# Who forms the first trial value of a threshold search, and where ScalarE's small copies stand

## What is computed

```python
def _top_p_attention(X, W1, W2, W3):
    q = X @ W1.T @ W2.T
    k = X @ W3.T
    probs = softmax(q @ k.T, axis=-1)                   # 4096 x 4096
    idx = argsort(-probs); sp = take_along_axis(probs, idx)
    keep_sorted = cumsum(sp) - sp < 0.9                 # the smallest set with 0.9 of the mass
    A = probs * mask                                    # mask: keep_sorted, put back in place
    return A / maximum(A.sum(-1), 1e-12)

R = (S + eye) / (S + eye).sum(-1)                       # S is adj
for n in range(2):
    A = _top_p_attention(Xa, W1, W2, W3)
    Xf = R @ Xf
    Xa = A @ Xa
    Z = Z + Xf @ U1[n].T + Xa @ U2[n].T
out = layernorm(x + layernorm(X + Z) * ln_g + ln_b)
```

## Time and profile before

| | us |
|---|---|
| median of 3 runs (4349.74 to 4353.28) | 4351.58 |
| the profiled execution | 4350.77 |
| its span | 4349.0 |
| busy in the span: TensorE | 3762.5 (87%) |
| VectorE | 3623.6 (83%) |
| ScalarE | 3114.5 (72%) |
| GpSimd | 1017.3 (23%) |

### The profile page before, as it was taken

One profiled execution on the slowest core, in us unless ns is written; L12 is line 12 of the kernel. 1 busy time (PEld: TensorE's weight loads), 2 busy tenths in 40 slices (PEclk: granted clock), 3 DMA queues, 4 the chain that ended last, 5 costly groups with the idle time before them and its releaser, 6 DMA issues.

```text
span 4349.0 us, 66313 instructions
## 1 busy us (share of the span) xinstructions
PE 3762.5 (87%) x25364; PEld 3163.1 (73%) x25364; DVE 3623.6 (83%) x6400; ACT 3114.5 (72%) x3128; POOL 1017.3 (23%) x1412
## 2 busy tenths in 40 slices
PE   8677877777777769999999749999999999999996
PEld 5677777777777747777778547777777777778875
DVE  2899999999999939888888188888888889999995
ACT  3789889898989845555555367777777777777771
POOL 0000000000000000001010224444444445555555
PEclk9899999999999989999999979999999999999998
DMA  3211111111111020000000212222233423333332
GB/s 116 93 45 66 45 55 56 47 64 47 64 47 64 27 78 12 19 16 19 16 17 17 87 35 85 87 83 88 88 93 93 134 90 105 107 107 105 100 104 73
DMA packets 131759, 292.49 MB, mean 67 GB/s; under 512 B 14122, under 2 KB 94186, under 8 KB 127058
## 3 DMA queue, kind: packets, MB, share of 16 engines
q1 hardware_dynamic: 131410, 287.99, 20.6%
HBM read 250.19 MB, written 37.75 MB: 66 GB/s over the span
## 4 chain that ended last, share of the span: by engine, by line
PE 34%; ACT 28%; DVE 14%; issue 14%; POOL 10%; DMA 1%; DVEq 0%; SPq 0%; ACTq 0%; POOLq 0%
PE ps L803 11%; PE ps L642 9%; DVE b L1226 7%; ACT b L871 6%; ACT b L988 5%; ACT b L989 5%; DVE b L1173 3%; ACT b L865 3%; PE ps L792 3%; ACT b L971 3%; PE ps L748 3%; PE ps L623 2%; POOL b L468 2%; ACT b L859 1%; PE ps L780 1%
## 5 line engine op out<-in xcount | busy, mean ns | idle before, releaser
L707 PE MATMUL ps<-b 128*128 128x257 f32 x4096 | 902.1, 379 | 0.0
L803 PE MATMUL ps<-b 128*128 128x257 f32 x4096 | 900.9, 379 | 0.0
L642 PE MATMUL ps<-cb,b 128*128 128x128 f32 x4096 | 606.9, 312 | 321.7 <-ACT b L865 321.7
L707 PEld LDWEIGHTS ps<-b 128*128 128x128 f32 x4096 | 775.6, 189 | 118.3 <-issue 3.8
L803 PEld LDWEIGHTS ps<-b 128*128 128x128 f32 x4096 | 770.2, 189 | 111.7
L642 PEld LDWEIGHTS ps<-cb,b 128*128 128x128 f32 x4096 | 546.1, 163 | 371.1 <-ACT b L865 329.6
L1137 DVE SCALAR_TENSOR_TENSOR b<-b 128x4096 f32<-128x4096 f32 x128 | 566.4, 4425 | 63.1 <-ACT b L859 59.8
L1139 DVE CUSTOM_DVE_ANT_0 b<-b 128x4096 f32<-128x4096 f32 x128 | 566.3, 4425 | 5.5 <-DMA b<-in_adj 1.1
L871 ACT ACTIVATE b<-ps 128x1024 f32<-128x1024 f32 x512 | 499.9, 1023 | 75.6 <-PE ps L642 74.0
L623 PE MATMUL ps<-b 128*64 128x128 f32 x8192 | 504.0, 276 | 0.0
L865 ACT ACTIVATE b<-b 128x4096 f32<-128x4096 f32 x128 | 474.4, 3706 | 8.0 <-DVE b L1141 8.0
(11 more groups left out here) (186 smaller groups left out, 4743.2 us busy)
## 6 DMA issues: line engine op xcount, KB each, us to landing
b<-in_adjTb SPq DMA_DIRECT2D x256, 512.0 KB, 3.8
b<-in_adj SPq DMA_DIRECT2D x32, 2048.0 KB, 8.0
y_d<-b SPq DMA_DIRECT2D x64, 128.0 KB, 1.7
h_d<-b SPq DMA_DIRECT2D x64, 128.0 KB, 1.8
b<-h_d SPq DMA_DIRECT2D x64, 128.0 KB, 2.3
b<-in_xT SPq DMA_DIRECT2D x1, 4096.0 KB, 15.8
b<-in_x SPq DMA_DIRECT2D x32, 128.0 KB, 2.2
b<-y_d SPq DMA_DIRECT2D x32, 128.0 KB, 2.1
```

Of the source, the lines that this page charges most:

```text
L642: last = nc.tensor.transpose(bank(2 * (gq % 3), 2)[:, b * 128:(b + 1) * 128], ub[:, u % UB, j * 128:(j + 1) * 128], ident_s)
L707: last = mm(b[:, 0:XA], aj[:, q % AJR, e, :], xf[:, j, :], start=False, stop=(j == NT - 1))
L803: last = mm(o[:, 0:XA], at[:, q % ATR, b, :], xa[:, j, :], start=(j == 0), stop=(j == NT - 1))
```

## The change

Three things, all in the second step:

- VectorE forms the product of the two bounds (`bracket_head`: three operations on 128x1), after the sixth level of tile `n` and ahead of the final rows' statistics; it waits for `e8` there and signals `bh`. With the `max` in it the choice between the two cases of the bracket is made in two operations.
- GpSimd's `bracket` begins with the root, once `bh` is there. Its own product (L474) goes. The bounds and the factors are computed after the root, as before. VectorE waits for the root (`bt`) ahead of L1232.
- ScalarE starts level 1 right after the exponentials; `av_ev` and `mq_ev` come between level 1 and level 2.

```diff
+LEAST = (1 - TOP_P) / 4096 / 1.0001
...
                 def bracket(t):
                     a = lambda i: ptm[:, i:i + 1]
                     Z = zE[:, t % 2:t % 2 + 1]
-                    po.wait_ge(g["e8"], t + 1)
+                    po.wait_ge(g["bh"], t + 1)
+                    m = tst[:, t % 2:t % 2 + 1]
+                    tt(m, m, ahalf, ALU.pow).then_inc(g["bt"], 1)
                     h7, g7 = e8[:, 7:8], am[:, 8:9]
                     ts(a(0), Z, TOP_P, None, ALU.mult)
...
-                    plink(tt(a(8), a(6), a(4), ALU.mult))
-                    tt(tst[:, t % 2:t % 2 + 1], a(8), ahalf, ALU.pow).then_inc(g["bt"], 1)
                     plink(tt(a(7), a(6), mone, ALU.pow))
...
-                def acts(t, items):
+                def acts(t, items, n):
                     items = list(items)
                     for k in range(1, ACT_LEVELS + 1):
                         if t < NT:
                             level(t, k)
+                        if k == 1:
+                            if 1 <= n <= NT:
+                                av_ev(n - 1)
+                            if n >= 2 or n + 2 < NT:
+                                mq_ev(n - 2 if n >= 2 else None, n + 2 if n + 2 < NT else None)
...
-                    if 1 <= n <= NT:
-                        av_ev(n - 1)
-                    if zm:
-                        mq_ev(tz, tx)
...
+                def bracket_head(t):
+                    Z = zE[:, t % 2:t % 2 + 1]
+                    ve.wait_ge(g["e8"], t + 1)
+                    link(v.scalar_tensor_tensor(out=x_, in0=Z, scalar=TOP_P, in1=am[:, 8:9], op0=ALU.mult,
+                                                op1=ALU.is_le))
+                    link(v.scalar_tensor_tensor(out=x_, in0=Z, scalar=LEAST, in1=x_, op0=ALU.mult, op1=ALU.max))
+                    v.tensor_scalar(tst[:, t % 2:t % 2 + 1], x_, e8[:, 7:8], None, ALU.mult).then_inc(g["bh"], 1)
...
                         if t == 0:
+                            bracket_head(0)
                             ve.wait_ge(g["bf"], 1)
...
+                        if t + 1 < NT:
+                            bracket_head(t + 1)
                         final_stats(t)
+                        if t + 1 < NT:
+                            ve.wait_ge(g["bt"], t + 2)
                         link(v.scalar_tensor_tensor(out=VN, in0=E, scalar=mid, in1=E, op0=ALU.is_le,
                                                     op1=ALU.mult, accum_out=G))
```

More of the change, by code:

```diff
@@ L273, in gat_topp_kernel @@
                       "gd", "po", "rd", "xs", "acc", "nz", "hi", "gi", "yd", "ys", "fi", "fa", "s1", "f1", "s2",
-                      "fo", "fd", "lv", "lr", "lt", "qd", "e8", "bt", "bf", "xc"):
+                      "fo", "fd", "lv", "lr", "lt", "qd", "e8", "bt", "bf", "xc", "bh"):
                 g[n] = sem(f"{n}_{s}")
@@ L468, in bracket @@
                     ts(a(1), h7, -1.0, 1.0, ALU.mult, ALU.add)
-                    plink(ts(a(2), Z, (1 - TOP_P) / 4096 / 1.0001, None, ALU.mult))
+                    plink(ts(a(2), Z, LEAST, None, ALU.mult))
                     ts(a(3), g7, a(0), None, ALU.is_ge)
@@ L1059, in _ @@
                         expo(n + 1)
-                    if 1 <= n <= NT:
-                        av_ev(n - 1)
-                    if zm:
-                        mq_ev(tz, tx)
[L1064 to L1067, removed]
+                    if s == 0:
+                        if 1 <= n <= NT:
+                            av_ev(n - 1)
+                        if zm:
+                            mq_ev(tz, tx)
+                        if tx is not None:
+                            gx_ev(tx)
+                    else:
+                        acts(n + 1, [2 * p + i for p in pairs_in(n) for i in range(2)], n)
                 barrier(ac, kS[s])
```

## The result

| | before | after |
|---|---|---|
| median of 5 runs, us | 4350.14 (4348.73 to 4353.28) | 4376.96 (4374.4 to 4378.75) |
| span of the profiled execution, us | 4349.0 | 4375.2 |
| ratio, 95% interval | | 1.0058 (1.0046 to 1.0070) |

The changed kernel is 0.6% slower. I had forecast 4340 us in a range of 4325 to 4370; the first rival, the lost race, stood at 4370, and the time lies 7 us above both.

The account below looks back on a forecast made before the run. No engine is full, so a loop of waits bounds the kernel (late, GpSimd's arrival at the reduction). Early -34 and late +22 give -12 us: 4339 from the profiled 4350.8, 4340 as median, range 4325 to 4370.

Parts of the forecast that it names:

- the first rival: Late periods: GpSimd's power operation L481 starts behind VectorE's L1232 and takes 6.45 us, not 2.31; +31, 4370 us; chance 0.22.
- the slower rival: Same as the first rival: late, L481 falls behind L1232, 12 periods cost 4.25 us instead of 1.9; 4370 us, chance 0.22.
- the early gain: Early periods: -5.6 + 1.6 + 2.1 = -1.9 us each, over 18 periods -34 us.
- root's path: Early: with VectorE's head and GpSimd's root first, ScalarE's levels start 1.64 us behind the exponentials, not 7.21; -5.6 us.
- copies: Early: ScalarE's three copies, free under the wait for the root, come onto the loop behind level 1; +1.6 us per period.
- ScalarE's stall: Early: ScalarE waits for the factors ahead of L995 because GpSimd is stopped by L1232; +2.1 us per period.
- the earlier trace: Rows of one late period before the change where L481 took 6.45 us; the forecast counted its loss as regained, -2.4 us.
- GpSimd stopped behind the root: Early: GpSimd's second small operation behind the root is held until VectorE's L1232 ends, taking more than 4 us.
- TensorE not the bound: Early: TensorE needs at most 53.3 us per period, less than the new period of 54.7.
- the border period: The period between the early and late regimes, where ScalarE was just last; +0.5 us.
- the late copy behind level 1: Late: the product's copy (L1010) delays GpSimd's L492 from 9.96 to 11.9 us behind the exponentials; +1.9 us, 12 periods, +23.
- The fast rival: Early: GpSimd isn't stopped behind the root, factors come in time; -58 to -72 instead of -34, 4302 to 4316 us; chance 0.1.

Follow-up runs that it names:

- e1: The changed kernel with two small VectorE operations added ahead of L1252 in the late turns; 4342.7 us.
- e7: The changed kernel with one small VectorE operation added ahead of L1252 in the late turns; 4337.8 us.
- e2: The changed kernel with the three ScalarE copies back ahead of level 1, leaving only the new way to the root; 4324.2 us.
- e6: The changed kernel with the three copies back ahead of level 1 and two small VectorE operations ahead of L1252 in the late turns; 4296.8 us.
- run 12: Not a follow-up run: part of the phrase "a race run 12 times", the race of L482 and L1252 in the last 12 periods.
- e3: The kernel before with only the three ScalarE copies moved behind level 1; 4425.9 us.
- e5: The changed kernel with VectorE, in turns before 17, starting L1252 only after GpSimd's signal just ahead of the power operation; 4358.7 us.
- e4: The kernel before with one more small GpSimd operation at the head of the bracket in the late turns; 4372.8 us.
- e8: e6 with GpSimd's search levels (its reduction) moved ahead of its work on the final rows; 4301.5 us.

## Why the prediction was wrong

**The step that failed** is the one in the slower rival, "By my sum L481 starts 4.25 us behind the start of the third head operation, and L1232 4.29", from which I had L481 just ahead. In the rows above it is 4.40 and 4.29 (L1222 3750.94, L482 3755.34, L1252 3755.23). VectorE's side was exact, and the root started at +0.30 as worked out. From the root to the power operation it took 4.10, not 3.95 us, and 0.11 of that lies in one place: the operation behind the root came 0.64 us after its start (3751.24 to 3751.88), where 0.53 stood between L475 and its follower in before. (With 0.53 the spacings of the row in before add up to the 3.95.) A sum of a dozen spacings was asked to decide an order by 0.04 us, and was 0.15 off. A margin that small gives near even odds, not 0.22. My range also ended at the rival's own number, 4370, and left nothing for an error in it. With the race won, by e1 and e7, the kernel takes 4342.7 and 4337.8 us, on both sides of my 4340; against the runs of before beside them that is 7 and 15 us faster, where I had forecast 12.

**The size of the rival.** It was put at 4370 and came out at 4377. The loop started 1.7 us later, where I had 0.6, but only 0.49 of that is the head's; the early gain was 31.1, not 34 (root's path -5.7, copies +1.7, ScalarE's stall +2.4, where I had -5.6, +1.6 and +2.1); and a late period lost 4.6 us instead of 4.25. One reading was off: in the earlier trace rows the factors came 2.2 us later behind the last exponential (by the start of L492, 12.15 against 9.96); 2.4 is their delay behind L1232's own start, which was 0.2 sooner there.

**Right:** the root's path, 0.92 us to the root and 1.50 to the levels (forecast 1.64 for the latter); GpSimd stopped behind the root, 4.53 us, though at its first small operation and not its second; early periods 54.96 us in the mean where I said 54.7; TensorE not the bound; the border period, +0.6 for +0.5; the late copy behind level 1, which e1 shows alone as L493 at 11.96 (forecast 11.9) and +1.8 us a period (forecast 1.9); the loss passing on to the reduction and VectorE's wait. The fast rival fell, since the stop behind the root came in every early period.

**What I didn't see.** First, GpSimd is held until the end of VectorE's operation whether the race is won or lost, so that winning it is worth the 2.3 us of the power operation at most. Second, the copies are better left where they were: I charged them 1.6 us early and took their place for needed; e2 and e6 show that ScalarE has the room, 4296.8 us against e1's 4342.7.

The row for the first, timeline of before, a late period, to be read with the earlier trace rows:

```profile
3771.30 2.19 POOL L482 TENSOR_SCALAR b<-b 128x2 f32<-128x2 f32 x1
```

L482 ends 0.09 us behind the end of L1232.

**Open:** why the operation behind the root comes after 0.64 us and not 0.53. In before the follower was a second power operation (L476), here it is a TENSOR_SCALAR (L470); no run varied it. Also open are the 0.6 us between GpSimd's arrival at the reduction and the answer (e1).

## What to carry to other kernels

Where two engines start long operations within some tenths of a microsecond and one of them can stop the other, treat the order as a term of its own: look for it in all periods of the trace, ask which edits upstream shift either side, and make it safe with an explicit wait or a cheap delay of the side that wins nothing by being early. Before work is moved off a wait that hides it, work out what the wait becomes once the thing waited for is sooner: here ScalarE still had to wait, only further down. Test the parts of a change by themselves: here one part alone gains 26 us, the other costs 46 to 76, and a tenth of a microsecond, in a race run 12 times, another 34.

## What the hardware showed

**A GpSimd operation that starts behind VectorE's is held until VectorE is done.** In the traces of all ten kernels, from 2480 us on, 861 GpSimd operations started 0.12 to 3.9 us behind the start of a VectorE 128x4096 two-input operation (SCALAR_TENSOR_TENSOR), and each of them took over 0.3 us more than the shortest one of its own line. The edge is sharp for the power operation: 0.50 to 0.00 us ahead (before, e1, e3, e5, e6, e7) it took its 2.31 us, 0.08 to 0.28 us behind (e2, after, e5, before, e4) 6.4 to 6.6. L470, 0.05 to 0.06 behind in the early periods of after, took 4.53. Closer than that the order isn't decided by the recorded starts: in e8, L528 started 0.01 us behind VectorE's L1237 and was held (4.81 us), and L540 started 0.04 behind and took its 0.73, while L1237 took 5.05 us instead of 4.49 (3803.86).

**The other way it depends on the GpSimd operation.** Behind the power operation VectorE loses nothing (3710.24 and 3710.38 in e6: 4.49 us as ever). Behind a 128x256 two-input operation it does. Timeline, changed kernel, an early period; the first row is the same VectorE line in a turn with nothing on GpSimd beside it:

```profile
2540.96 0.32 DVE L1279 TENSOR_TENSOR_SCAN b<-b 128x48 f32<-128x48 f32 x1
...
2867.48 0.74 POOL L507 TENSOR_TENSOR b<-b 128x256 f32<-128x256 f32 x1
2867.65 0.68 DVE L1279 TENSOR_TENSOR_SCAN b<-b 128x48 f32<-128x48 f32 x1
```

L1279 starts 0.17 us behind L507, takes 0.68 instead of 0.32 us, and ends 0.11 behind it. The Trainium skill (SBUF — State Buffer, "Who interferes with whom") has the second one to issue block fully; the trace agrees for GpSimd as the second and for VectorE behind a 128x256 operation, and does not for VectorE behind the power operation. Why the power operation is different, no run shows.

**TensorE's clock, and when the product comes.** In the period of before read above, TensorE waits 3.23 us, works at first at 2.4 GHz, and is then granted 1.2. Windows of before, TensorE (stretch, us, busy, granted clock, DMA share, GB/s):

```profile
2842.18:2844.18 2.00, 0.27 (x2) 1.00 0.00 0
2844.18:2846.18 2.00, 2.00 (x12) 0.73 0.00 0
2846.18:2848.18 2.00, 2.00 (x6) 0.50 0.00 0
```

In e2 the wait is 1.29 us in most early periods and the clock stays at 2.4 GHz from 2600 to 3400 us. A window of e2, TensorE, and behind it its rows in the timeline:

```profile
2877.80:2879.80 2.00, 2.00 (x14) 1.00 0.00 0
```

```profile
2824.35 1.09 PE L793 MATMUL ps<-cb,b 128*128 128x128 f32 x8 [1.29 <-ACT b L1052]
2825.38 3.77 PE L749 MATMUL ps<-kr 64*128 64x512 f32 x16
```

The same work in before, first two periods ahead of the windows, then in their period:

```profile
2730.78 1.09 PE L792 MATMUL ps<-cb,b 128*128 128x128 f32 x8 [3.07 <-ACT b L1051]
2731.80 3.77 PE L748 MATMUL ps<-kr 64*128 64x512 f32 x16
...
2844.94 5.40 PE L748 MATMUL ps<-kr 64*128 64x512 f32 x16
```

The length of the wait alone doesn't decide it: behind 3.07 us here the clock stayed at 2.4 GHz, and behind 2.05 us (3070.24) it fell. What it costs can be read inside before. In the three early periods in which these 16 matmuls take 3.77 us (from 2731.80, 2958.13 and 3354.13), the next product comes 1.11 us behind the last exponential, as in e2; in the four in which they take 5.40 (from 2844.94, 3127.84, 3240.99 and 3524.01), at 2.70 to 2.76. The 1.6 us are the same on both sides. So the sooner product of e2, which I had missed, is the clock's. That e2 keeps the clock because its wait is shorter is argued, not shown: no run varied the wait alone.
